# Statistics of x by sums on ScalarE, gate and value products in two-part form, v spread a step later

## The chip, the cores and the metric

One NeuronCore of a Trainium2 chip. The metric is the device time of one execution in microseconds. The kernel before was run three times: 274.16, 274.37 and 275.07 us, median 274.37 us.

## What is computed

x is (4, 1024, 256) in fp32. One layer of linear attention and one of a gated channel mix, each on a layer norm:

```python
a = layernorm(x)                                  # no gain, no bias
q = a @ Wq + bq;  k = (a @ Wk + bk) @ Wc @ We;  v = (a @ Wv + bv) @ Wc @ We
qf, kf = elu(q) + 1, elu(k) + 1                   # 16 heads of 16, 4 heads for k and v
num = qf . cumsum(kf outer v);  den = qf . cumsum(kf) + 1e-6
y = a + (num / den) @ Wo + bo
x2 = x + layernorm(y) * gamma + beta
z = layernorm(x2);  zp = z one token earlier (0 for the first)
xr = mu_r*z + (1-mu_r)*zp;  xk = mu_k*z + (1-mu_k)*zp
out = x2 + sigmoid(xr @ W_r) * (relu(xk @ W_k)**2 @ W_v)
```

## The kernel before

Tokens go in 8 chunks of 128 tokens; a chunk takes the same 128 positions of all 4 batches, so the tiles have 128 tokens on the partitions and 4 x 256 values (or, transposed, 128 of 256 channels on the partitions and 512 tokens). Each engine has its own list of instructions, written out by hand; semaphores tie them together. After a prologue for weights and chunk 0, `step(c)` runs for c = 0 to 6 and `finale(7)` closes. In one step four chunks are in flight:

- n + 1 = c + 2: `norm_x`, the statistics of x (`bn_stats` and `bn_aggr` on DVE, L1053 and L1059), rstd and bias on POOL (L233 to L237), then `normalise_x` on ACT (L890, `a_tok`);
- n = c + 1: `a_tok` is transposed and copied out (`aT`), keys and values (L418, `kb`, `v_half`), the queries (L431, L434), the feature map exp(min(q,0)) on ACT (`eq`, L844 and L846) and its max on DVE (`qf`, L1089), the sums of keys (`ksum`), the products for the denominators on POOL (`prod`, L284);
- c: scores, mask (`probs`, L1125), outputs and division (`oT`, L1137);
- m = c - 1: output projection (L514), residual and statistics of y (`y_tok`), `centre` (L1158), `second_residual` (L1169, writes `x2_tok`), its statistics, then `normalise_z` on ACT (L904);
- f = c - 2: the channel mix: `shift_z` (`zT`), the difference `dz` on POOL (L292), `xr` and `xk` on DVE (L1184), `mix_r` (L536) with `gate_r` (tanh on ACT), `mix_k` (L529) with `channel_k` (relu, square, `ka_high` on ACT), `mix_v_parts` (L567, L571), the gate on DVE (L1197), `finish` on POOL (L299), and the store.

A product of two fp32 matrices is either one fp32 matmul per tile (two instructions each in the trace), or three fp32r matmuls: an operand is split into a high part (a copy that rounds, on ACT) and a low part (operand minus high part, on DVE or POOL), and high x high, high x low and low x high are summed. Before, the queries of chunks 2 to 7, the value product `mix_v` in the steps and for the last chunk, and `mix_r` of the last chunk are done in parts; `mix_r` of the others is fp32.

Steps 0 and 1 are shorter (no channel mix yet). POOL's `add_bo` and `add_beta` (L269, L276) prepare what the residuals add. The middle of a step on ACT, the engine that the change loads, reads

```python
                if n + 1 < NC:
                    normalise_x(n + 1)
                keys(n)
                if f >= 0:
                    gate_r(f, 0, x1)
                ...
                queries(n, 0, x0)
                queries(n, 1, x1)
                values(n)
                state_blocks(n)
```

Here `values(n)` spreads `v_half` over the heads (`v_pad`, four copies), `state_blocks` copies the running state, and `keys_transposed` makes `kfT`, for which the next chunk's first scores wait.

## Time and profile before

| | |
|---|---|
| median of 3 runs | 274.37 us |
| the profiled execution, its own time | 275.64 us |
| its span | 273.9 us |
| granted TensorE clock over the span | 0.994 |
| PE busy | 261.3 us (95%), 3035 matmuls |
| DVE busy | 233.0 us (85%), 561 |
| ACT busy | 164.9 us (60%), 331 |
| POOL busy | 146.4 us (53%), 167 |
| DMA | 10.75 MB, mean 39 GB/s |
| chain that ended last | PE 62%, DVE 20%, ACT 10%, issue 5%, POOL 2% |

Times in the rows are microseconds from the start of the span. "busy" is time in which an engine works on an instruction; the chain that ended last is the row of instructions, each released by the one before it, that leads to the end. PE's matmuls overlap, so starts are read rather than durations. Step 0 lies at about 23 to 43 us, step 1 to 65, step 2 to 98, steps 3 to 6 follow at about 30 us each, and the finale begins at 219 us.

### The profile page before, as it was taken

The page shows a single profiled execution, that of the slowest core. Times are in us where ns is not written, and L with a number is a line of the kernel's source. Part 1 is how long each engine was busy: PE and PEld are TensorE (multiplying, and loading weights), DVE is VectorE, ACT ScalarE, POOL GpSimd, SP SyncE. Part 2 cuts the span into 40 slices and gives each one's busy share as a digit, 9 for nine tenths or more (in the row PEclk, how much of TensorE's full clock was granted, in tenths as well). Part 3 has the DMA queues.
Part 4 walks back from the last instruction along what each step waited for, and adds up shares of the span by engine and source line. Part 5 has one row for each costly group of instructions (what it writes and reads, how often), then busy time and mean ns, then how long its engine had stood idle before and what let it go on. Part 6 is the DMA issues. An engine that isn't in the chain of part 4 may idle for free.

```text
span 273.9 us, 7728 instructions
## 1 busy us (share of the span) xinstructions
PE 261.3 (95%) x3035; PEld 197.0 (72%) x3035; DVE 233.0 (85%) x561; ACT 164.9 (60%) x331; POOL 146.4 (53%) x167
## 2 busy tenths in 40 slices
PE   7999999999898999999999999999999999999894
PEld 7867657868675588758886688658875777685763
DVE  6759578979799989898999989997899877999494
ACT  2448696695746965486747965586438820354670
POOL 3545495579683678335833686355533624070542
PEclk9889999999999999999999999999999999999999
DMA  5910220000020022000400020001100020000213
GB/s 166 274 66 1 79 67 15 4 2 0 4 77 2 2 90 67 2 1 7 151 0 2 2 79 1 0 5 41 41 0 4 2 79 2 0 0 0 78 41 116
DMA packets 12180, 10.75 MB, mean 39 GB/s; under 512 B 2288, under 2 KB 12144, under 8 KB 12144
## 3 DMA queue, kind: packets, MB, share of 16 engines
q1 hardware_dynamic: 11392, 9.97, 11.5%
q8 instruction: 24, 0.39, 0.6%
q10 hardware_dynamic: 752, 0.30, 0.4%
q14 instruction: 12, 0.10, 0.1%
HBM read 6.07 MB, written 4.19 MB: 37 GB/s over the span
## 4 chain that ended last, share of the span: by engine, by line
PE 62%; DVE 20%; ACT 10%; issue 5%; POOL 2%; DVEq 0%; POOLq 0%; ACTq 0%
PE ps_x L514 7%; PE ps_x L529 7%; PE ps_x L536 6%; PE ps_x L418 5%; PE ps_z L485 5%; PE ps_y L501 4%; PE ps_y L506 4%; PE ps_x L567 4%; DVE xk L1184 4%; PE ps_z L589 3%; DVE stats L1053 3%; DVE qf L1089 2%; PE ps_x L522 2%; ACT eq L844 2%; PE ps_x L571 2%
## 5 line engine op out<-in xcount | busy, mean ns | idle before, releaser
L1125 DVE TENSOR_TENSOR probs<-ps_z,causal 128x1024 f32<-128x1024 f32 x32 | 38.7, 1210 | 2.5 <-PE ps_z L485 2.2
L276 POOL TENSOR_TENSOR xb_tok<-x_in,beta_bc 128x1024 f32<-128x1024 f32 x8 | 19.5, 2443 | 20.7 <-DVE x_tok L1169 20.7
L514 PE MATMUL ps_x<-wo_sb,oT 128*128 128x256 f32 x128 | 30.0, 382 | 0.0
L299 POOL TENSOR_TENSOR out_tok<-tanh_r,x_tok 128x512 f32<-128x512 f32 x14 | 18.3, 1315 | 20.1 <-DVE tanh_r L1197 19.8
L284 POOL TENSOR_TENSOR prod<-qf,ksum 128x1024 f32<-128x1024 f32 x7 | 16.5, 2363 | 23.4 <-DVE ksum L1098 23.4
L269 POOL TENSOR_TENSOR abo_tok<-a_tok,bo_bc 128x1024 f32<-128x1024 f32 x8 | 19.1, 2382 | 15.0 <-DVE prod L1118 6.0
L514 PEld LDWEIGHTS ps_x<-wo_sb,oT 128*128 128x128 f32 x128 | 23.4, 190 | 3.6 <-issue 0.5
L485 PE MATMUL ps_z<-qf,kfT 32*128 32x128 f32 x512 | 23.3, 296 | 1.9 <-ACT rden_bc L824 1.1
L229 POOL TENSOR_TENSOR rstd<-rstd,neg_half 128x4 f32<-128x4 f32 x23 | 23.9, 1038 | 1.8
L485 PEld LDWEIGHTS ps_z<-qf,kfT 32*128 32x128 f32 x512 | 17.2, 185 | 7.5 <-issue 3.2
L501 PE MATMUL ps_y<-qf,state 32*32 32x128 f32 x512 | 20.5, 274 | 1.0 <-DVE oT L1137 0.4
L501 PEld LDWEIGHTS ps_y<-qf,state 32*32 32x32 f32 x512 | 11.9, 104 | 12.4 <-issue 9.0
L506 PE MATMUL ps_y<-probs,v_pad 128*32 128x128 f32 x512 | 20.6, 279 | 0.0
L529 PE MATMUL ps_x<-xk,wkT 128*128 128x512 f32 x40 | 18.5, 605 | 1.3 <-DVE qf L1089 1.0
L904 ACT ACTIVATE z_tok<-x_tok,nbias,rstd 128x256 f32<-128x256 f32 x32 | 16.6, 591 | 4.5 <-POOL nbias L237 4.5
L292 POOL TENSOR_TENSOR dz<-zT 128x512 f32<-128x512 f32 x14 | 14.5, 1059 | 7.6 <-ACT zT L824 7.5
L536 PE MATMUL ps_x<-wrT,xr 128*128 128x256 f32 x80 | 18.1, 379 | 0.0
L890 ACT ACTIVATE a_tok<-x_in,nbias,rstd 128x256 f32<-128x256 f32 x24 | 12.5, 590 | 8.7 <-POOL nbias L237 4.4
L418 PE MATMUL ps_x<-wkv_sb,aT 128*128 128x128 f32 x128 | 17.5, 294 | 0.0
L844 ACT ACTIVATE eq<-ps_x,neg_bq 128x512 f32<-128x512 f32 x15 | 10.3, 684 | 11.8 <-PE ps_x L434 11.3
L418 PEld LDWEIGHTS ps_x<-wkv_sb,aT 128*128 128x128 f32 x128 | 16.2, 205 | 0.8
L1089 DVE SCALAR_TENSOR_TENSOR qf<-ps_x,bq,eq 128x512 f32<-128x512 f32 x15 | 11.2, 746 | 6.5 <-ACT eq L846 6.5
(184 smaller groups left out, 668.1 us busy)
## 6 DMA issues: line engine op xcount, KB each, us to landing
x_in<-in_L_attn_x_dram SPq DMA_DIRECT2D x8, 512.0 KB, 4.2
out_dram<-out_tok SPq DMA_DIRECT2D x16, 256.0 KB, 2.1
xr<-in_L_attn_Wq_dram ACTq DMA_DIRECT2D x1, 256.0 KB, 4.2
xk<-in_L_ffn_W_r_dram SPq DMA_DIRECT2D x1, 256.0 KB, 5.1
xk<-in_L_ffn_W_k_dram SPq DMA_DIRECT2D x1, 256.0 KB, 5.3
xr<-in_L_ffn_W_v_dram SPq DMA_DIRECT2D x1, 256.0 KB, 5.6
wo_sb<-in_L_attn_Wo_dram SPq DMA_DIRECT2D x4, 64.0 KB, 4.9
bo_bc<-in_L_attn_bo_dram SPq DMA_DIRECT2D x1, 128.0 KB, 5.3
```

What stands on the lines that cost most here:

```text
L229: PL.tensor_tensor(dst[:], dst[:], neg_half[:], ALU.pow).then_inc(done, 1)
L269: PL.tensor_tensor(abo_tok[n % 2][:], a_tok[n % 2][:], bo_bc[:].unsqueeze(1).to_broadcast([P, NB, D]), ALU.add).then_inc(s_ab, 1)
L276: PL.tensor_tensor(xb_tok[n % 2][:], x_in[n % XBUF][:], beta_bc[:].unsqueeze(1).to_broadcast([P, NB, D]), ALU.add).then_inc(s_xb, 1)
L299: PL.tensor_tensor(out_tok[:, 2 * i:2 * i + 2, :], tanh_r[:, i].rearrange("p (b d) -> p b d", b=2), x2_tok[m % 3][:, 2 * i:2 * i + 2, :], ...
L418: last = mm(x0[:, b * P:(b + 1) * P], aT[:, k, b * P:(b + 1) * P], wkv_sb[:, k, :], start=(k == 0), stop=(k == KD - 1))
L485: last = mm(ps_z[:, g, u * P:(u + 1) * P], kfT[c % 2][rows, 2 * b + u, :, :], qf[c % 2][rows, :, t0:t0 + HALF], start=True, stop=True, ski ...
L501: mm(ps_y[rows, off + u * P:off + (u + 1) * P], state[rows, slot, b, :, :], qf[c % 2][rows, :, t0:t0 + HALF], start=(u == 0), stop=False, ...
L506: last = mm(ps_y[32 * g:32 * g + 32, off + u * P:off + (u + 1) * P], v_pad[c % 2][:, b, u, g, :, :], probs[b % 2][:, g, u * P:(u + 1) * P] ...
L514: last = mm(bk_[:, (b % 2) * D:(b % 2 + 1) * D], oT[m % 2][:, a, b, :], wo_sb[:, a, :], start=(a == 0), stop=(a == 1))
L529: last = mm(bk_[:, :], wkT[:, k, n * P:(n + 1) * P], xk[:, k, :, :], start=(k == 0), stop=(k == KD - 1))
L536: last = mm(bk_[:, (b % 2) * D:(b % 2 + 1) * D], xr[:, k, b, :], wrT[:, k, :], start=(k == 0), stop=(k == KD - 1))
L1125: V.tensor_tensor(probs[b % 2][:].rearrange("p g (r s) -> p g r s", s=HALF), ps_z[:, :, 0:2 * P].rearrange("p g (r s) -> p g r s", s=HALF) ...
```

## The change

- **x's statistics.** In steps 2 to 5 (chunks 4 to 7) DVE's `norm_x` goes. ACT makes them: `sums_x`, four copies of x into `a_tok` with an accumulated sum; POOL's `mean_x`; `squares_x`, four `Square` activations with the mean as bias and an accumulated sum, in two pairs; POOL's `scale_x`; then `normalise_x`, now behind the queries. `values` of chunks 3 to 6 moves to the next step, ahead of `sums_x`; step 6 does chunk 7's as before.
- **Two-part products.** `mix_r` of chunks 0 to 4 (now `mix_r_parts`, with `high_xr` on ACT and `low_xr` on DVE, in buffers of their own), `mix_v` of chunk 6, and the queries of chunk 1. `wq_high` and `wq_low` are made in the prologue.
- **Key features.** exp(min(k,0)) is now two activations, relu and exp; DVE's min goes.
- **Denominators.** The addition of 1e-6 moves from DVE to ACT from step 2 on. `prod` is made in two halves and shares `eq`'s buffer.
- **Prologue.** `a_tok` of chunk 1 is scaled on ACT (two rows before, two after `keys(0)`) and no more on DVE; the transposes of chunk 0 stand together.
- **Order.** In step 0 ACT does the keys before `normalise_x` and `kfT` before the state; in steps 2 to 6 DVE does the second query half before the second `xk`; in step 2 the reciprocals are spread before the second half of the projection.
- **Output.** The sum is written into `x2_tok`, `out_tok` goes; SP waits for the store before.
- **Finale.** Chunk 7's `second_residual`, statistics and scale are done in two halves, its transposes stand before `mix_v` of chunk 6, and its `dz` and `xk` alternate.

The diff, its core (indentation cut by 12):

```diff
@@ -90,7 +93,7 @@
-prod = sb("prod", 2, T)
+prod = eq
@@ -104,7 +107,8 @@
-xr_p, wr_split, s_xrh, s_xrl = aT_p, sem("wr_split"), sem("xr_high"), sem("xr_low")
+xr_p = [ctx.enter_context(nc.sbuf_tensor(f"xr_{part}", [P, KD, T], F32R)) for part in ("high", "low")]
+wr_split, s_xrh, s_xrl = sem("wr_split"), sem("xr_high"), sem("xr_low")
@@ -188,8 +193,10 @@
+        if m >= 1:
+            sp.wait_ge(out_stored[i], 16 * m)
 ...
-                     out_tok[:, 2 * i:2 * i + 2, :]).then_inc(out_stored[i], 16)
+                     x2_tok[m % 3][:, 2 * i:2 * i + 2, :]).then_inc(out_stored[i], 16)
@@ -241,6 +248,21 @@
+def mean_x(n):
+    pool.wait_ge(s_a, 4 * n)
+    pool.wait_ge(s_xs, 4 * (n - 3))
+    PL.tensor_tensor(neg_mean0[:], sum0[:], neg_share[:], ALU.mult)
+    PL.tensor_tensor(mean16[:], sum0[:], neg_share16[:], ALU.mult).then_inc(s_nb0, 1)
+
+def scale_x(n):
+    pool.wait_ge(s_xq, 4 * (n - 3))
+    PL.tensor_tensor(rstd0[:], sq0[:], ln_eps[:], ALU.add).then_inc(s_rs0, 1)
+    pool.wait_ge(s_rs0, 2 * n + 1)
+    PL.tensor_tensor(rstd0[:], rstd0[:], neg_half[:], ALU.pow).then_inc(s_rs0, 1)
+    pool.wait_ge(s_rs0, 2 * n + 2)
+    pool.wait_ge(s_nb0, 2 * n + 1)
+    PL.tensor_tensor(nbias0[:], neg_mean0[:], rstd0[:], ALU.mult).then_inc(s_nb0, 1)
+
@@ -281,8 +303,8 @@
-    PL.tensor_tensor(prod[:], qf[n % 2][:], flat(ksum[n % 2]).unsqueeze(1).to_broadcast([P, 2, T]),
-                     ALU.mult).then_inc(s_prod, 1)
+    for a in range(2):
+        PL.tensor_tensor(prod[:, a, :], qf[n % 2][:, a, :], flat(ksum[n % 2]), ALU.mult).then_inc(s_prod, 1)
@@ -294,23 +316,23 @@
         pool.wait_ge(s_gt, 2 * m + i + 1)
-        if m >= 1:
-            pool.wait_ge(out_stored[i], 16 * m)
-        PL.tensor_tensor(out_tok[:, 2 * i:2 * i + 2, :], tanh_r[:, i].rearrange("p (b d) -> p b d", b=2),
+        PL.tensor_tensor(x2_tok[m % 3][:, 2 * i:2 * i + 2, :], tanh_r[:, i].rearrange("p (b d) -> p b d", b=2),
                          x2_tok[m % 3][:, 2 * i:2 * i + 2, :], ALU.add).then_inc(s_out, 1)
 ...
         token_difference(f)
-    if n + 1 < NC:
+    if f < 0:
         norm_x(n + 1)
-    if f == 0:
-        add_beta(n - 1)
     if f >= 0:
 ...
         first_norm(m)
+        if n + 1 < NC:
+            mean_x(n + 1)
         add_beta(n)
+        if n + 1 < NC:
+            scale_x(n + 1)
         denominator_terms(n)
@@ -322,14 +344,13 @@
             add_beta(n)
-            pool.wait_ge(wq_split, 1)
-            PL.tensor_tensor(wq_p[1][:], wq_sb[:], wq_p[0][:].bitcast(F32), ALU.subtract).then_inc(wq_split, 1)
             pool.wait_ge(wr_split, 1)
 ...
             add_bo(n)
+            add_beta(n)
         else:
@@ -343,13 +364,23 @@
-    second_norm(c)
+    for h in range(2):
+        rows = slice(2 * h, 2 * h + 2)
+        pool.wait_ge(s_st2, 8 * c + 4 * h + 4)
+        if h == 0:
+            pool.wait_ge(s_z, 4 * c)
+        PL.tensor_tensor(neg_mean2[:, rows], mv2[:, rows, 0], neg_one[:, rows], ALU.mult).then_inc(s_nb2, 1)
+        PL.tensor_tensor(rstd2[:, rows], mv2[:, rows, 1], ln_eps[:, rows], ALU.add).then_inc(s_rs2, 1)
+        pool.wait_ge(s_rs2, 2 * c + 2 * h + 1)
+        PL.tensor_tensor(rstd2[:, rows], rstd2[:, rows], neg_half[:, rows], ALU.pow).then_inc(s_rs2, 1)
+        pool.wait_ge(s_rs2, 2 * c + 2 * h + 2)
+        pool.wait_ge(s_nb2, 2 * c + 2 * h + 1)
+        PL.tensor_tensor(nbias2[:, rows], neg_mean2[:, rows], rstd2[:, rows], ALU.mult).then_inc(s_nb2, 1)
 ...
-        pool.wait_ge(out_stored[i], 16 * c)
-        PL.tensor_tensor(out_tok[:, 2 * i, :], tanh_r[:, i, 0:D], x2_tok[c % 3][:, 2 * i, :],
+        PL.tensor_tensor(x2_tok[c % 3][:, 2 * i, :], tanh_r[:, i, 0:D], x2_tok[c % 3][:, 2 * i, :],
@@ -389,6 +422,8 @@
+pool.wait_ge(wq_split, 1)
+PL.tensor_tensor(wq_p[1][:], wq_sb[:], wq_p[0][:].bitcast(F32), ALU.subtract).then_inc(wq_split, 1)
@@ -637,10 +672,10 @@
+    pe.wait_ge(s_pr, 8 * c + 2)
+    spread_reciprocals(c, (z0, z1, z2, z3))
 ...
-    pe.wait_ge(s_pr, 8 * c + 2)
-    spread_reciprocals(c, (z0, z1, z2, z3))
@@ -648,27 +683,22 @@
         pe.wait_ge(s_y, 2 * m + (1 if f else 2))
-        mix_r(f, 0, x1)
+        pe.wait_ge(wr_split, 2)
+        mix_r_parts(f, 0, x1)
         pe.wait_ge(s_y, 2 * m + 2)
-        mix_r(f, 1, x2)
+        mix_r_parts(f, 1, x2)
     outputs(c, 0)
 ...
     pe.wait_ge(s_kv, 2 * n + 2)
-    if m >= 0:
-        pe.wait_ge(wq_split, 2)
-        query_parts(n, 0, x0)
-    else:
-        queries(n, 0, x0)
+    pe.wait_ge(wq_split, 2)
+    query_parts(n, 0, x0)
     if f >= 0:
 ...
         pe.wait_ge(ffn_w_sb, 1)
-    if m >= 0:
-        query_parts(n, 1, x1)
-    else:
-        queries(n, 1, x1)
+    query_parts(n, 1, x1)
     outputs(c, 1)
@@ -747,20 +777,20 @@
     pe.wait_ge(s_zT, 2 * m + 2)
+    transpose_z(c, x0, x2)
     pe.wait_ge(s_gt, 2 * f + 1)
-    mix_v(m, 0, x1)
-    transpose_z(c, x0, x2)
+    mix_v_parts(m, 0, x1)
     pe.wait_ge(s_gt, 2 * f + 2)
-    mix_v(m, 1, ps_y)
+    mix_v_parts(m, 1, ps_y)
     pe.wait_ge(s_rl, 2 * m + 1)
 ...
     pe.wait_ge(wr_split, 2)
-    mix_r_parts(0, z2)
+    mix_r_parts(c, 0, z2)
     pe.wait_ge(s_th, 2 * m + 2)
-    mix_r_parts(1, z3)
+    mix_r_parts(c, 1, z3)
     pe.wait_ge(s_gt, 2 * m + 1)
@@ -833,7 +863,9 @@
-    AC.activation(ek[:], kb[:], ACT.Exp).then_inc(s_ek, 1)
+    AC.activation(ek[:], kb[:], ACT.Relu, scale=-1.0).then_inc(s_nk, 1)
+    act.wait_ge(s_nk, n + 1)
+    AC.activation(ek[:], ek[:], ACT.Exp, scale=-1.0).then_inc(s_ek, 1)
@@ -859,6 +892,11 @@
+def guarded_denominators(n):
+    act.wait_ge(s_den_ps, n + 1)
+    act.wait_ge(s_rb_ps, n)
+    copy(rden[:], x0[:, 0:P], bias=DEN_EPS).then_inc(s_den, 1)
+
@@ -880,13 +918,27 @@
-def normalise_x(n):
+def sums_x(n):
+    act.wait_ge(x_loaded[n % XBUF], x_value(n))
+    act.wait_ge(s_aT_ps, 2 * n - 2)
+    act.wait_ge(s_ab, n - 1)
+    act.wait_ge(s_nb0, 2 * n)
+    for b in range(NB):
+        copy(a_tok[n % 2][:, b, :], x_in[n % XBUF][:, b, :], accum_out=sum0[:, b:b + 1]).then_inc(s_xs, 1)
+
+def squares_x(n, rows):
+    act.wait_ge(s_nb0, 2 * n + 1)
+    for b in rows:
+        AC.activation(a_tok[n % 2][:, b, :], x_in[n % XBUF][:, b, :], ACT.Square, bias=mean16[:, b:b + 1],
+                      scale=1.0 / 16, accum_out=sq0[:, b:b + 1]).then_inc(s_xq, 1)
+
+def normalise_x(n, rows=range(NB)):
 ...
-    for b in range(NB):
+    for b in rows:
@@ -923,6 +977,13 @@
+
+def high_xr(m):
+    if m >= 1:
+        act.wait_ge(s_r_ps, 2 * m)
+    for k in range(KD):
+        act.wait_ge(s_xr, 2 * m + k + 1)
+        copy(xr_p[0][:, k, :], xr[:, k].rearrange("p b t -> p (b t)")).then_inc(s_xrh, 1)
@@ -944,37 +1005,58 @@
         copy(flat(wrT), x1[:, :]).then_inc(ffn_w_sb, 1)
+    if c in (0, 2):
+        reciprocals(c)
+    if f >= 0:
+        high_xr(f)
+    for k in range(KD):
+        act.wait_ge(s_aT, 2 * n + k + 1)
+        copy(aT_p[0][:, k, :], aT[:, k, :]).then_inc(s_aTh, 1)
+    if c == 1:
+        reciprocals(c)
+    on_act = 2 <= c and n + 1 < NC
+    if c == 0:
+        keys(n)
+    if c >= 3:
+        values(c)
+    if on_act:
+        sums_x(n + 1)
+    elif n + 1 < NC:
+        normalise_x(n + 1)
     if c >= 1:
-        for k in range(KD):
-            act.wait_ge(s_aT, 2 * n + k + 1)
-            copy(aT_p[0][:, k, :], aT[:, k, :]).then_inc(s_aTh, 1)
-    if c <= 2:
-        reciprocals(c)
-    if n + 1 < NC:
-        normalise_x(n + 1)
-    keys(n)
+        keys(n)
     if f >= 0:
         gate_r(f, 0, x1)
+    if on_act:
+        squares_x(n + 1, (0, 1))
     if c == 1:
 ...
     if c == 0:
-        copy(flat(wq_p[0]), flat(wq_sb)).then_inc(wq_split, 1)
         act.wait_ge(ffn_w_sb, 1)
 ...
         gate_r(f, 1, x2)
+    if on_act:
+        squares_x(n + 1, (2, 3))
     queries(n, 0, x0)
     queries(n, 1, x1)
-    values(n)
-    state_blocks(n)
+    if on_act:
+        normalise_x(n + 1)
+    else:
+        values(n)
     if c == 0:
 ...
         copy(flat(wkT), x1[:, :]).then_inc(ffn_w_sb, 1)
+        keys_transposed(n)
+    state_blocks(n)
     if f >= 0:
 ...
         channel_k(f, 1, x0, True)
-    keys_transposed(n)
+    if f >= 0:
+        guarded_denominators(n)
+    if c >= 1:
+        keys_transposed(n)
     if c == 0:
@@ -993,15 +1075,13 @@
-    channel_k(m, 0, z0)
-    channel_k(m, 1, z1)
+    channel_k(m, 0, z0, True)
+    channel_k(m, 1, z1, True)
 ...
-    for k in range(KD):
-        act.wait_ge(s_xr, 2 * c + k + 1)
-        copy(xr_p[0][:, k, :], xr[:, k].rearrange("p b t -> p (b t)")).then_inc(s_xrh, 1)
+    high_xr(c)
@@ -1027,8 +1107,12 @@
+act.wait_ge(wq_ready, 1)
+copy(flat(wq_p[0]), flat(wq_sb)).then_inc(wq_split, 1)
+normalise_x(1, (0, 1))
 ...
+normalise_x(1, (2, 3))
@@ -1105,10 +1189,11 @@
-    dve.wait_ge(s_den_ps, n + 1)
-    if n >= 1:
-        dve.wait_ge(s_rb_ps, n)
-    V.tensor_scalar(rden[:], x0[:, 0:P], DEN_EPS, None, ALU.add).then_inc(s_den, 1)
+    if n < 3:
+        dve.wait_ge(s_den_ps, n + 1)
+        if n >= 1:
+            dve.wait_ge(s_rb_ps, n)
+        V.tensor_scalar(rden[:], x0[:, 0:P], DEN_EPS, None, ALU.add).then_inc(s_den, 1)
@@ -1158,13 +1243,13 @@
-def second_residual(m):
+def second_residual(m, rows=range(NB)):
 ...
-        dve.wait_ge(s_out, 2 * m - 4)
-        dve.wait_ge(s_z, 4 * m - 8)
-    for b in range(NB):
+        dve.wait_ge(out_stored[0], 16 * (m - 2))
+        dve.wait_ge(out_stored[1], 16 * (m - 2))
+    for b in rows:
@@ -1203,19 +1287,18 @@
         reciprocal(0)
-    if n + 1 < NC:
+    if f < 0:
         norm_x(n + 1)
-    if f < 0:
         short_step(c, n, m)
 ...
         add_residual(m, 0, x1)
-        add_residual(m, 1, x1)
     token_shift(f, 0, *for_r)
 ...
         add_residual(m, 0, x1)
-        add_residual(m, 1, x2)
+    low_xr(f)
+    add_residual(m, 1, x2 if f else x1)
     mask(c, 1)
@@ -1226,8 +1309,8 @@
     token_shift(f, 0, *for_k)
+    queries(n, 1, x1)
     token_shift(f, 1, *for_k)
-    queries(n, 1, x1)
     divide(c, 1)
@@ -1243,8 +1326,16 @@
-        dve.wait_ge(s_aTh, 2 * n - 3 + k)
+        dve.wait_ge(s_aTh, 2 * n - 1 + k)
 ...
+
+def low_xr(m):
+    if m >= 1:
+        dve.wait_ge(s_r_ps, 2 * m)
+    for k in range(KD):
+        dve.wait_ge(s_xrh, xr_value(m) - 1 + k)
+        V.tensor_tensor(xr_p[1][:, k, :], xr[:, k].rearrange("p b t -> p (b t)"), xr_p[0][:, k, :].bitcast(F32),
+                        ALU.subtract).then_inc(s_xrl, 1)
@@ -1260,8 +1351,10 @@
     else:
-        keys_values(n)
+        keys_values(n, (0,))
         mask(c, 1)
+        keys_values(n, (1,))
+        low_a(n)
     key_features(n)
@@ -1306,19 +1399,24 @@
-    second_residual(c)
-    second_stats(c)
+    for h in range(2):
+        rows = (2 * h, 2 * h + 1)
+        second_residual(c, rows)
+        if h == 0:
+            dve.wait_ge(s_nb2, 2 * c)
+        dve.wait_ge(s_x2, 4 * c + 2 * h + 2)
+        row_stats(x2_tok[c % 3], stats2, s_st2, 8 * c, rows)
+        row_means(stats2, mv2, s_st2, 8 * c + 4 * h, rows)
+    low_part(m, 0)
+    low_part(m, 1)
 ...
-    token_difference(c)
-    token_shift(c, 0, *for_k)
-    token_shift(c, 1, *for_k)
+    for k in range(KD):
+        token_difference(c, k)
+        token_shift(c, k, *for_k)
 ...
-    for k in range(KD):
-        dve.wait_ge(s_xrh, k + 1)
-        V.tensor_tensor(xr_p[1][:, k, :], xr[:, k].rearrange("p b t -> p (b t)"), xr_p[0][:, k, :].bitcast(F32),
-                        ALU.subtract).then_inc(s_xrl, 1)
+    low_xr(c)
@@ -1369,7 +1466,6 @@
-norm_x_scale(1)
```

How the lists read. ACT in step 4 (chunk 4 in attention, statistics for chunk 6) from the high part of aT to the last eq. Before:

```order
L824 ACTIVATE aT_high<-aT 128x512 x2
L890 ACTIVATE a_tok0<-x_in0,nbias0,rstd0 128x256 x4
L836 ACTIVATE ek<-kb 128x256
L824 ACTIVATE v_half<-v_half 64x4x64
L931 ACTIVATE tanh_r<-ps_x1 128x512
L824 ACTIVATE kf<-kf 128x16x16
L931 ACTIVATE tanh_r<-ps_x2 128x512
```

After, the same stretch:

```order
L854 ACTIVATE aT_high<-aT 128x512 x2
L854 ACTIVATE v_pad0<-v_half 64x4x4x16 x4
L854 ACTIVATE a_tok0,sum0<-x_in0 128x256 x4
L866 ACTIVATE ek<-kb 128x256
L868 ACTIVATE ek<-ek 128x256
L854 ACTIVATE v_half<-v_half 64x4x64
L992 ACTIVATE tanh_r<-ps_x1 128x512
L932 ACTIVATE a_tok0,sq0<-x_in0,mean16 128x256 x2
L854 ACTIVATE kf<-kf 128x16x16
L992 ACTIVATE tanh_r<-ps_x2 128x512
L932 ACTIVATE a_tok0,sq0<-x_in0,mean16 128x256 x2
```

The scaling of x has left, and v_pad, the sums, the squares and a second activation for ek have come in.

ACT in step 4 behind the queries. Before:

```order
L844 ACTIVATE eq<-ps_x1,neg_bq 128x512
L846 ACTIVATE eq<-eq 128x512
L824 ACTIVATE v_pad1<-v_half 64x4x4x16 x4
L824 ACTIVATE state<-tail1,row_mask 128x4x16 x4
L920 ACTIVATE k_act<-ps_x1 128x512
L922 ACTIVATE k_act<-k_act 128x512
```

After:

```order
L877 ACTIVATE eq<-ps_x1,neg_bq 128x512
L879 ACTIVATE eq<-eq 128x512
L942 ACTIVATE a_tok0<-x_in0,nbias0,rstd0 128x256 x4
L854 ACTIVATE state<-tail1,row_mask 128x4x16 x4
L974 ACTIVATE k_act<-ps_x1 128x512
L976 ACTIVATE k_act<-k_act 128x512
```

v_pad's place between the queries and the state is taken by the scaling of x, which needs nbias from POOL.

POOL in step 4, from the token difference to the products for the denominators. Before:

```order
L292 TENSOR_TENSOR dz<-zT 128x512 x2
L233 TENSOR_TENSOR neg_mean0<-mv0,neg_one 128x4
L227 TENSOR_TENSOR rstd0<-mv0,ln_eps 128x4
L229 TENSOR_TENSOR rstd0<-rstd0,neg_half 128x4
L237 TENSOR_TENSOR nbias0<-neg_mean0,rstd0 128x4
L269 TENSOR_TENSOR abo_tok1<-a_tok1,bo_bc 128x1024
L227 TENSOR_TENSOR rstd1<-mv1,ln_eps 128x4
L229 TENSOR_TENSOR rstd1<-rstd1,neg_half 128x4
L276 TENSOR_TENSOR xb_tok1<-x_in2,beta_bc 128x1024
```

After:

```order
L314 TENSOR_TENSOR dz<-zT 128x512 x2
L291 TENSOR_TENSOR abo_tok1<-a_tok1,bo_bc 128x1024
L234 TENSOR_TENSOR rstd1<-mv1,ln_eps 128x4
L236 TENSOR_TENSOR rstd1<-rstd1,neg_half 128x4
L254 TENSOR_TENSOR neg_mean0<-sum0,neg_share 128x4
L255 TENSOR_TENSOR mean16<-sum0,neg_share16 128x4
L298 TENSOR_TENSOR xb_tok1<-x_in2,beta_bc 128x1024
L259 TENSOR_TENSOR rstd0<-sq0,ln_eps 128x4
L261 TENSOR_TENSOR rstd0<-rstd0,neg_half 128x4
L264 TENSOR_TENSOR nbias0<-neg_mean0,rstd0 128x4
```

nbias of x stood ahead of abo_tok; it now stands behind xb_tok.

## Rows read from the trace of the kernel before

**Rows 1.** Stretches: busy time (and count) of PE, PEld, DVE, ACT, POOL; clock, DMA
```profile
68.00:98.70 30.70, 28.20 (x355) 20.39 (x353) 27.65 (x65) 20.94 (x43) 18.51 (x18) 1.00 0.06 19
129.00:159.30 30.30, 30.10 (x371) 22.84 (x370) 28.06 (x69) 20.42 (x41) 17.45 (x18) 1.00 0.11 36
```

**Rows 2.** The chain that ended last, step 4: start, duration, what
```profile
128.35 0.66 PE ps_z L485 x16
...
137.89 3.46 PE ps_x L536 x16
...
153.86 0.44 DVE oT L1137
...
155.55 0.67 PE ps_x L567 x4
...
158.61 0.66 PE ps_z L485 x16
```

**Rows 3.** Timeline of ACT, step 4: start, duration, instructions [idle before]
```profile
138.66 0.42 ACT L836 ACTIVATE ek<-kb 128x256 f32<-128x256 f32 x1 [1.12 <-DVE kb L1075]
...
144.77 0.69 ACT L844 ACTIVATE eq<-ps_x,neg_bq 128x512 f32<-128x512 f32 x1 [2.56 <-PE ps_x L434]
...
147.39 1.72 ACT L824 ACTIVATE v_pad<-v_half 64x256 f32<-64x256 f32 x4
149.45 1.06 ACT L824 ACTIVATE state<-tail,row_mask 128x64 f32<-128x64 f32 x4 [0.35 <-DVE tail L1104]
150.97 0.60 ACT L920 ACTIVATE k_act<-ps_x 128x512 f32<-128x512 f32 x1 [0.45 <-PE ps_x L529]
...
154.07 0.63 ACT L824 ACTIVATE ka_high<-k_act 128x512 fp32r<-128x512 f32 x1
```

**Rows 4.** Timeline of DVE, step 4
```profile
130.34 1.39 DVE L1053 BATCH_NORM_STATS2 stats<-x_in 128x6 f32<-128x256 f32 x4
...
132.07 1.88 DVE L1184 SCALAR_TENSOR_TENSOR xr<-dz,mu_r_col,zT 128x512 f32<-128x512 f32 x2
...
140.45 0.28 DVE L1080 TENSOR_SCALAR ek<-ek 128x256 f32<-128x256 f32 x1
...
141.19 1.29 DVE L1247 TENSOR_TENSOR aT_low<-aT,aT_high 128x512 fp32r<-128x512 f32 x2
142.40 1.67 DVE L1169 SCALAR_TENSOR_TENSOR x_tok<-y_tok,rstd,xb_tok 128x256 f32<-128x256 f32 x4
...
146.16 0.75 DVE L1089 SCALAR_TENSOR_TENSOR qf<-ps_x,bq,eq 128x512 f32<-128x512 f32 x1 [0.63 <-ACT eq L846]
```

**Rows 5.** Timeline of POOL, step 4
```profile
130.69 2.04 POOL L292 TENSOR_TENSOR dz<-zT 128x512 f32<-128x512 f32 x2 [0.17 <-ACT zT L824]
132.69 0.65 POOL L233 TENSOR_TENSOR neg_mean<-mv,neg_one 128x4 f32<-128x4 f32 x1
...
144.14 2.39 POOL L276 TENSOR_TENSOR xb_tok<-x_in,beta_bc 128x1024 f32<-128x1024 f32 x1 [4.40 <-DVE x_tok L1169]
...
153.47 0.20 POOL L227 TENSOR_TENSOR rstd<-mv,ln_eps 128x4 f32<-128x4 f32 x1
153.76 1.02 POOL L229 TENSOR_TENSOR rstd<-rstd,neg_half 128x4 f32<-128x4 f32 x1
```

**Rows 6.** Timeline of ACT, prologue and step 1
```profile
17.94 0.69 ACT L844 ACTIVATE eq<-ps_x,neg_bq 128x512 f32<-128x512 f32 x1 [0.40 <-PE ps_x L424]
...
53.87 2.07 ACT L896 ACTIVATE y_tok<-y_tok,nbias,rstd 128x256 f32<-128x256 f32 x4
```

**Rows 7.** Timeline of PE, steps 0 and 2
```profile
41.72 0.73 PE L485 MATMUL ps_z<-qf,kfT 32*128 32x128 f32 x16 [0.43 <-ACT kfT L824]
...
88.43 3.70 PE L529 MATMUL ps_x<-xk,wkT 128*128 128x512 f32 x8 [1.00 <-DVE qf L1089]
```

**Rows 8.** Timeline of PE and of DVE, finale
```profile
260.04 3.67 PE L529 MATMUL ps_z<-xk,wkT 128*128 128x512 f32 x8 [0.99 <-DVE xk L1184]
...
257.94 1.29 DVE L1190 TENSOR_TENSOR dz<-zT 128x512 f32<-128x512 f32 x2 [3.91 <-ACT zT L824]
```

69 lines of the change are left out of this document (38 added, 31 removed).

## The prediction

> **What bounds the kernel now.** I read the stretches first, to see which engine has room. In steady step 4 PE is busy for 30.1 of 30.3 us, DVE for 28.1, ACT for 20.4 and POOL for 17.5; in step 2 PE is busy for 28.2 of 30.7 [rows 1]. So two engines are nearly full, and ACT has some 10 us of room. The chain of waits then says what a step's length is made of: from one `scores(n,0)` at 128.35 to the next at 158.61 it is 30.26 us, almost all PE, with a detour over ACT and DVE in the middle and one over the division `oT` at 153.86 ahead of the last outputs [rows 2]. PE is the bound, but DVE has one idle gap of 0.63 us in the first 17 us of the step, before `qf` [rows 4]. A gain on PE beyond about that is worth what DVE, ACT and POOL let through. The timelines of ACT, DVE and POOL in step 4 are read for that: what is free, what waits for whom [rows 3 to 5]. The prologue, step 2 and the finale bind elsewhere: ACT's `eq` releases `qf` after the prologue's queries, in step 2 PE stands 1.00 us for DVE's `qf`, in the finale 0.99 us for `xk` [rows 6 to 8].
>
> I forecast the difference by positions in the profiled execution (275.64 us; span 273.9) and apply it to the median, 274.37, which lies 1.27 below.
>
> **Steady steps 3, 4, 5, in step 4's times.**
>
> PE: 16 instructions of `mix_r` take 3.46 us in the chain. The value product in parts, same shape, 24 instructions, takes from 155.55 to 158.61, 3.06 [rows 2]. Gain 0.40 a step, if nothing is in the way.
>
> DVE loses x's statistics (1.39 and some 0.35 for the means, [rows 4]) and min (0.28, with a wait 0.4). It gains `low_xr`, priced like `aT_low`, 1.29. But the 1.7 us at the front are not all won: `xr` needs `dz`, whose two halves end at about 131.7 and 132.7 [rows 5]. So the second `xr` ends at 133.5 instead of 133.95 (from 132.07, 1.88, [rows 4]), and 1.3 us of `low_xr` follow. The mask of block 1 and `kb` come 0.9 late, `kf` and `aT_low` 0.5, and `second_residual` ends at 144.5 instead of 144.07. The idle 0.63 before `qf` then swallows the rest: `qf` 0 starts at about 145.95, 0.2 earlier than now. From there to the division that releases the last outputs nothing changes but the order of `qf` and `xk`. DVE alone would thus let a step end 0.0 to 0.3 us earlier, not 0.40.
>
> ACT gains `xr_high` 2 x 0.6, a second activation for `ek` (0.42), the addition for the denominators (about 0.25), and eight passes over x. No row shows an activation with an accumulated sum. The lower bound is a plain one of this size, 2.07 / 4 = 0.52 a piece, less overlap [rows 6]; `v_pad` is 0.43 a piece [rows 3]. An upper bound is one and a half times that, 0.75. I take 0.52, since the arithmetic per element is that of the row. Then ACT runs: aT_high to 135.3, v_pad to 137.0, sums to 139.0, keys (`kb` is there at 139.5) to 140.65, tanh to 141.2, squares, kf, tanh and squares to 144.4, and the first `eq` can start at 144.4, where PE releases it at 144.77 - 0.4 [rows 3]. It just fits. This is 6 us of added work at a cost of nothing, covered by ACT's idle 1.12 before `ek` and 2.56 before `eq` [rows 3] and others; without that cover each 0.1 us lands on `qf` directly.
>
> The Trainium skill (ScalarE: Activation LUTs, Rules for kernel authors) says that relu, max, min and add belong on VectorE, not on ScalarE. By that rule the moved min and addition are a loss; here the row has 0.28 on DVE and 0.42 on ACT, so the rule agrees in size, but in steps 3 to 6 the trace gives ACT room for it.
>
> POOL and ACT behind the queries: this is where I see the loss. `normalise_x` now stands between the queries and the state copies, and waits for nbias. `scale_x` stands behind `xb_tok` on POOL, and `xb_tok` starts when `second_residual` ends: 144.14 now, right after 144.07 [rows 4, 5]. After the change: x_tok ends 144.5, `xb_tok` 144.55 to 147.0. Then an addition (0.20), pow (1.02) and a product (0.20) with gaps, 1.6 us [rows 5], give 148.6. But the small ones are slower when DVE works from SBUF: 0.65 instead of 0.20 beside `xr` [rows 5]. The addition falls beside `xk`, so I take 148.6 to 149.4, middle 149.0. ACT then does four scalings, 2.07 [rows 6], to 151.1, the state (1.06, less overlap 1.0) to 152.1, and the chain from `k_act` to `ka_high`, 150.97 to 154.70 [rows 3], 3.7 us, to 155.7. Before it was done at 154.70. `mix_v_parts` waits for it: 155.7 instead of 155.55, and the second `ka_low` (0.64) comes after it, while PE needs it 0.55 after its start: another 0.1 to 0.2. So a step is 0.1 to 0.7 longer: I take **+0.35 us, three times, +1.05**.
>
> The Trainium skill (SBUF — State Buffer, SBUF: two separate sides) says that VectorE with two SBUF inputs and GpSimd lock each other out for a whole instruction. By it `xk`, wanted at 146.6, would wait for `xb_tok`'s end at 147.0, and POOL's addition for `xk`; nbias would come at 149.3 and the step would be 0.5 longer. The row of 0.65 agrees.
>
> **Step 2.** No statistics of x on DVE, `low_xr` instead, and the second `y_tok` only after it; `centre` no longer beside POOL's two long additions. I place the start of `mix_k`, now 88.43 after 1.00 us of standing [rows 7], 1.5 us earlier. But `xb_tok`, `scale_x`, `normalise_x`, state and `channel_k` follow as above: second residual 83.35, `xb_tok` 85.8, nbias 87.8, `ka_high` 94.6. PE's value product starts at 94.96 in the same timeline before, and at 94.7 to 95.0 after. **-0.1.**
>
> **Step 6** has no statistics of x. PE's 0.40 are the limit, DVE has `low_xr` more and min less: **-0.4.**
>
> **Prologue and steps 0, 1.** ACT does, between `keys(0)` and `queries(0)`, two scalings (1.04) and the relu (0.42). It ended `v_half` at 17.54 and started `eq` at 17.94, released by PE [rows 6]. Now it is free at 16.73 + 0.42 + 0.42 + 0.32 + 1.04 = 18.9, less overlap 18.8: +0.86 on `qf`, and all of it on the chain, as `qf`, `ksum`, `qf` and `prod` follow each other on DVE. In step 0 some comes back: no `wq_high` ahead of `eq`, and `kfT` ahead of the state (1.06), which counts since `kfT` releases `scores(1,0)` at 41.72 [rows 7]. I come to 42.2: **+0.5.** In step 1 relu and exp of the keys stand ahead of the scaling of y at 53.87 on ACT [rows 6], which the chain goes through: **+0.4.**
>
> **Finale.** `mix_k` of the last chunk waited 0.99 us for `xk` to 260.04; `dz` took 257.94 to 259.23, then both `xk` [rows 8]. Now chunk 7's z is scaled in halves, its last transpose is done at about 256.5 instead of 257.3, and the first `xk` needs only the first `dz`. `mix_v` of chunk 6 in parts costs ACT 1.3 and DVE 1.3, both beside other work, and ends at 259.35. So `mix_k` starts at 259.4: **-0.6.** The store is behind the last sum as before; SP's new wait is for a store that is 2 us old by then.
>
> Sum: 0.9 - 0.1 + 1.05 - 0.4 - 0.6 = **+0.85, 275.2 us**. What else moves costs nothing where other work covers it: `prod` in halves (same sum; PE's first denominators start earlier, not the last), the queries of chunk 1 in parts (PE was not last in step 0), the sum in place (the store read the same bytes).
>
> **The rivals.**
>
> *It becomes faster, since ACT and POOL are not last.* If POOL's three small instructions run undisturbed and the plain copies overlap better than I count, nbias comes at 148.4 and `ka_high` at 155.1, and DVE's `oT` sets the step: -0.3 each in steps 3 to 5, -1.0 in step 2. Sum 0.9 - 1.0 - 0.9 - 0.4 - 0.6 = -2.0: **272.4**. It decides the sign as soon as `ka_high` ends before PE's last outputs, some 155.1. For it speaks ACT's 10 us of room [rows 1], against it that the chain over POOL has no slack at all in my count.
>
> *No change.* nbias at 148.6, steps 3 to 5 at 0.0 to +0.15, step 2 at -0.3: **274.2**.
>
> *Accumulated sums cost more.* At 0.75 a piece, sums and squares take 1.8 us more, of which 0.5 hides before `kb`; `eq` comes 0.8 to 1.3 late, and so does everything behind `qf`. Four steps at +0.9 instead of the above: **278**. For it: no row shows the price.
>
> *The stored chunks hold DVE up.* `second_residual` now waits for the store of the chunk three earlier. That store is asked for at the end of step m - 1 and lands some 2 us later, while it is needed 15 us into a later step; I give it 0.02 within the last case.
>
> **Chances.** Forecast case 0.40 (own range 274.7 to 276.5; a quarter of it lies below 275.19), no change 0.22, faster 0.26, costly sums 0.12. A measurement of this kernel can tell about 0.3% from no change, that is 273.55 to 275.19. So slower 0.30 + 0.12 = 0.42, within 0.10 + 0.21 = 0.31, faster 0.26 + 0.01 = 0.27 (0.01 of the no-change case lies below 273.55). Range: from the faster case to most of the costly one, 272.2 to 277.4.
>
> **What would show it.** In the new timeline: ACT's `a_tok` with nbias in step 4 idles for POOL for about 2 us behind the last `eq` (right), or starts at once (the faster rival). `ka_high` ends some 27 us after the step's mask starts at 129.2, now 25.5 after. `eq` of the first query half released by PE (right) or straight behind a square (costly sums; also their mean above 0.6 us). `mix_r` 0.4 shorter. The first `qf` after the prologue at 20.2 instead of 19.32. `mix_k` of the last chunk without its 0.99 of idle. The prediction is wrong if the steps 3 to 5 are shorter than 30.2 us.

## The result and the profile after

| | before | changed |
|---|---|---|
| median of the runs timed together | 274.71 us (274.16 to 275.07) | 278.63 us (278.38 to 278.73) |
| ratio, 95% interval | | 1.0142 (1.0120 to 1.0164) |
| profiled execution, its span | 275.64, 273.9 us | 278.73, 276.3 us |

Slower by 3.9 us, where I had forecast 0.85 slower and a range that ended at 277.4. The starts of `scores(c, 0)` on PE give the time by step:

| | prologue | 0 | 1 | 2 | 3 | 4 | 5 | 6 | finale |
|---|---|---|---|---|---|---|---|---|---|
| before | 22.86 | 18.86 | 21.45 | 34.85 | 30.26 | 30.26 | 30.26 | 30.25 | 54.86 |
| changed | 21.52 | 18.45 | 21.88 | 35.08 | 31.35 | 31.33 | 31.33 | 30.30 | 55.08 |
| difference | -1.34 | -0.41 | +0.43 | +0.23 | +1.09 | +1.07 | +1.07 | +0.05 | +0.22 |

So 3.2 us lie in steps 3, 4 and 5. The busy time of the changed kernel's steps 2 and 4 (us; PE, PEld, DVE, ACT, POOL; clock), beside [rows 1]:

```profile
67.00:97.60 30.60, 28.07 (x362) 20.07 (x359) 26.04 (x58) 23.75 (x58) 19.36 (x19) 1.00 0.06 19
129.00:160.30 31.30, 29.86 (x378) 22.63 (x377) 27.08 (x60) 25.32 (x61) 18.55 (x20) 1.00 0.12 36
```

PE is no longer full: it has 29.9 us of work in 31.3, DVE 27.1, ACT 25.3. The step has become longer than any engine's work, so waits make it. The chain of waits of step 4, where [rows 2] had almost only PE:

```profile
131.84 0.94 DVE xr L1269
...
135.32 1.19 DVE xr_low L1337 x2
136.51 0.61 DVE y_tok L1233
...
137.27 2.39 POOL abo_tok L291
...
140.89 0.45 POOL neg_mean L254
141.33 1.95 POOL mean L255
...
145.19 0.98 ACT a_tok L932 x4
146.17 0.58 ACT eq L877
...
155.41 0.64 PE ps_y L536 x16
```

It runs over DVE, POOL (`mean`), ACT (the squares, then `eq`) and reaches PE only at the end. POOL, step 4 (start, duration, instruction, [idle before]):

```profile
140.89 0.45 POOL L254 TENSOR_TENSOR neg_mean<-sum,neg_share 128x4 f32<-128x4 f32 x1
141.29 1.98 POOL L255 TENSOR_TENSOR mean<-sum,neg_share 128x4 f32<-128x4 f32 x1
144.88 2.37 POOL L298 TENSOR_TENSOR xb_tok<-x_in,beta_bc 128x1024 f32<-128x1024 f32 x1 [1.60 <-DVE x_tok L1254]
...
148.58 0.33 POOL L264 TENSOR_TENSOR nbias<-neg_mean,rstd 128x4 f32<-128x4 f32 x1
```

DVE at the same time, beside [rows 4]:

```profile
131.84 2.09 DVE L1269 SCALAR_TENSOR_TENSOR xr<-dz,mu_r_col,zT 128x512 f32<-128x512 f32 x2 [1.42 <-POOL dz L314]
133.86 0.68 DVE L1233 TENSOR_TENSOR y_tok<-ps_x,abo_tok 128x512 f32<-128x512 f32 x1
...
140.01 1.66 DVE L1243 SCALAR_TENSOR_TENSOR y_tok<-y_tok,mv,gamma_bc 128x256 f32<-128x256 f32 x4
141.59 0.42 DVE L1167 SCALAR_TENSOR_TENSOR kf<-kb,ek 128x256 f32<-128x256 f32 x1
141.93 1.29 DVE L1330 TENSOR_TENSOR aT_low<-aT,aT_high 128x512 fp32r<-128x512 f32 x2
...
147.44 0.75 DVE L1173 SCALAR_TENSOR_TENSOR qf<-ps_x,bq,eq 128x512 f32<-128x512 f32 x1 [1.18 <-ACT eq L879]
```

and ACT, beside [rows 3]:

```profile
137.29 0.42 ACT L854 ACTIVATE a_tok<-x_in 128x256 f32<-128x256 f32 x1
137.61 0.19 ACT L854 ACTIVATION_READ_ACCUMULATOR a_tok<-x_in 128x1 f32 x1
137.70 0.40 ACT L854 ACTIVATE a_tok<-x_in 128x256 f32<-128x256 f32 x1
...
143.31 0.51 ACT L932 ACTIVATE a_tok<-x_in,mean 128x256 f32<-128x256 f32 x1 [1.86 <-POOL mean L255]
...
146.07 0.67 ACT L877 ACTIVATE eq<-ps_x,neg_bq 128x512 f32<-128x512 f32 x1
...
148.99 2.08 ACT L942 ACTIVATE a_tok<-x_in,nbias,rstd 128x256 f32<-128x256 f32 x4 [0.35 <-POOL nbias L264]
...
153.73 0.58 ACT L974 ACTIVATE k_act<-ps_x 128x512 f32<-128x512 f32 x1
```

Three things are to be seen. A POOL instruction on 128x4 elements takes 1.98 us: it begins while DVE goes from `centre` over `kf` to `aT_low` without a gap, and ends at 143.27, about when `aT_low` does. ACT stands 1.86 us for it. And `eq` starts directly behind the last square, not released by PE as at 144.77 before. The price of the sums is not the matter: from one to the next it is 0.40 us, of the squares 0.50, the read of the accumulator (0.19) included.

### The profile page after: what moved, and what is told of

Same layout as the page of the kernel before. It is cut to its first block, busy times and chain, and to the rows that moved or that the text cites. A ratio compares the mean times of both kernels' runs of the same rounds, so it can differ in the third digit from the quotient of the medians.

```text
span 276.3 us, 7926 instructions
## 1 busy us (share of the span) xinstructions
PE 258.0 (93%) x3087; PEld 195.5 (71%) x3087; DVE 228.9 (83%) x523; ACT 191.3 (69%) x426; POOL 153.6 (56%) x184
## 4 chain that ended last, share of the span: by engine, by line
DVE 39%; POOL 18%; PE 17%; ACT 13%; issue 11%; DVEq 0%; POOLq 0%; ACTq 0%
DVE stats L1137 6%; POOL abo_tok L291 4%; DVE ksum L1182 4%; DVE xr L1269 4%; POOL x_tok L319 4%; DVE xk L1269 3%; DVE y_tok L1233 3%; DVE probs L1210 3%; POOL mean L255 3%; PE ps_z L624 3%; ACT a_tok L932 2%; PE ps_x L602 2%; DVE xr_low L1337 2%; POOL dz L314 2%; DVE oT L1222 2%
## 5 line engine op out<-in xcount | busy, mean ns | idle before, releaser
L319 POOL TENSOR_TENSOR x_tok<-tanh_r,x_tok 128x512 f32<-128x512 f32 x14 | 18.3, 1311 | 19.7 <-DVE tanh_r L1281 19.7
L307 POOL TENSOR_TENSOR eq<-qf,ksum 128x512 f32<-128x512 f32 x14 | 17.6, 1278 | 20.1 <-DVE ksum L1182 20.1
L298 POOL TENSOR_TENSOR xb_tok<-x_in,beta_bc 128x1024 f32<-128x1024 f32 x8 | 18.9, 2368 | 10.4 <-DVE x_tok L1254 10.4
L1269 DVE SCALAR_TENSOR_TENSOR xr<-dz,mu_r_col,zT 128x512 f32<-128x512 f32 x16 | 14.7, 960 | 7.3 <-POOL dz L314 7.3
L536 PEld LDWEIGHTS ps_y<-qf,state 32*32 32x32 f32 x512 | 11.9, 104 | 11.2 <-issue 5.5
L236 POOL TENSOR_TENSOR rstd<-rstd,neg_half 128x4 f32<-128x4 f32 x18 | 18.6, 1034 | 1.4
L942 ACT ACTIVATE a_tok<-x_in,nbias,rstd 128x256 f32<-128x256 f32 x28 | 14.6, 589 | 3.4 <-POOL nbias L244 2.1
L854 ACT ACTIVATE zT<-ps_x 128x512 f32<-128x512 f32 x16 | 8.7, 595 | 11.8 <-PE ps_x L557 11.7
L541 PEld LDWEIGHTS ps_y<-probs,v_pad 128*32 128x32 f32 x512 | 12.0, 109 | 6.3 <-issue 6.1
L453 PE MATMUL ps_x<-wkv_sb,aT 128*128 128x128 f32 x128 | 16.4, 281 | 0.0
```

The source lines that it names most:

```text
L236: PL.tensor_tensor(dst[:], dst[:], neg_half[:], ALU.pow).then_inc(done, 1)
L298: PL.tensor_tensor(xb_tok[n % 2][:], x_in[n % XBUF][:], beta_bc[:].unsqueeze(1).to_broadcast([P, NB, D]), ALU.add).then_inc(s_xb, 1)
L319: PL.tensor_tensor(x2_tok[m % 3][:, 2 * i:2 * i + 2, :], tanh_r[:, i].rearrange("p (b d) -> p b d", b=2), x2_tok[m % 3][:, 2 * i:2 * i + 2 ...
L536: mm(ps_y[rows, off + u * P:off + (u + 1) * P], state[rows, slot, b, :, :], qf[c % 2][rows, :, t0:t0 + HALF], start=(u == 0), stop=False, ...
L541: last = mm(ps_y[32 * g:32 * g + 32, off + u * P:off + (u + 1) * P], v_pad[c % 2][:, b, u, g, :, :], probs[b % 2][:, g, u * P:(u + 1) * P] ...
L1269: V.scalar_tensor_tensor(out=dst[:, k], in0=dz[:, k], scalar=mu[:, k:k + 1], in1=zT[:, k, :, 0:P], op0=ALU.mult, op1=ALU.add).then_inc(don ...
```

## The experiments

Position in step 4, in us after its `scores(4, 0)` began, for the kernels the argument rests on (differences of starts read to 0.01 from the timelines; "2nd relu" is the second relu of `k_act`, "step" the length of step 4):

| kernel | kb | mean took | eq | qf | nbias | state | 2nd relu | mix_v | step |
|---|---|---|---|---|---|---|---|---|---|
| before | 9.93 | | 16.49 | 17.88 | 6.90 | 21.17 | 24.51 | 27.20 | 30.26 |
| changed | 11.07 | 1.98 | 17.79 | 19.16 | 20.30 | 22.69 | 25.45 | 28.27 | 31.33 |
| e1, x undone | 11.08 | | 15.90 | 17.90 | 6.90 | 21.43 | 24.21 | 27.24 | 30.30 |
| e2, x alone | 9.93 | 0.64 | 16.50 | 17.89 | 19.60 | 22.10 | 24.87 | 27.22 | 30.28 |
| e8, mix_r undone | 9.93 | 1.98 | 16.65 | 18.02 | 19.20 | 21.56 | 24.38 | 27.14 | 30.21 |
| e3, mean on ACT | 11.07 | ACT | 15.89 | 17.90 | 20.76 | 23.03 | 25.81 | 28.16 | 31.22 |
| e9, beta late | 11.07 | 1.98 | 17.80 | 19.17 | 19.34 | 22.47 | 25.24 | 28.28 | 31.33 |
| e10, both | 11.07 | ACT | 15.90 | 17.89 | 17.74 | 21.19 | 23.97 | 27.01 | 30.08 |
| e11, both on POOL | 11.07 | 0.20 | 15.89 | 17.89 | 17.75 | 21.19 | 23.98 | 27.01 | 30.07 |

### Which part costs

**e1.** All of x put back in steps 2 to 5: `norm_x` on POOL and DVE, `normalise_x` and `values` where they were.

> The changed kernel with all that concerns x in steps 2 to 5 put back: its statistics on DVE and POOL, its scaling and v_pad where they were; everything else of the change stays. If the loss lies in x's statistics on ACT, by whatever mechanism, steps 3 to 5 (start to start of scores(c, 0)) fall from 31.3 us to 30.3 or less, and the time from 278.6 to 275.4 or less: 273.8 if the shorter mix_r (0.4 us a step) then shows, 275.4 if it is hidden. If the loss lies in another part (the order of DVE's pieces, mix_r in parts, prod in eq's buffer), it stays above 277.

274.08 us, 0.9975 (0.9960 to 0.9990) of before; steps 3 to 5 at 30.30 to 30.31. Without x's part there is no loss, and nothing of the shorter `mix_r` shows. DVE's `kb` comes at 11.08 as in the changed kernel: the statistics stood in the wait for `dz`.

```profile
128.29 1.40 DVE L1121 BATCH_NORM_STATS2 stats<-x_in 128x6 f32<-128x256 f32 x4
...
130.02 1.87 DVE L1253 SCALAR_TENSOR_TENSOR xr<-dz,mu_r_col,zT 128x512 f32<-128x512 f32 x2
131.82 0.68 DVE L1217 TENSOR_TENSOR y_tok<-ps_x,abo_tok 128x512 f32<-128x512 f32 x1
```

The first `y_tok` stands 5.59 us into the step with the statistics on DVE and 5.58 without (131.82 - 126.23; 133.86 - 128.28). Taking them away won nothing at this point.

**e2.** The kernel before with x's part alone.

```diff
-                if n + 1 < NC:
+                on_act = 2 <= c and n + 1 < NC
+                if c >= 3:
+                    values(c)
+                if on_act:
+                    sums_x(n + 1)
+                elif n + 1 < NC:
                     normalise_x(n + 1)
 ...
-                values(n)
+                if on_act:
+                    normalise_x(n + 1)
```

> The kernel before with only x's part of the change: sums and squares on ACT in steps 2 to 5, the scaling behind the queries, v_pad in the next step. If x's part alone carries the loss: steps 3 to 5 about 31.3 us instead of 30.3, step 6 as before, 278.0 to 279.0 us in all. If it only hurts together with the rest (high_xr's two passes on ACT as well), steps 3 to 5 stay within 0.4 us of 30.3 and the time below 276.5.

277.34 us, 1.0095 (1.0075 to 1.0115): between my two bounds, and neither case holds: steps 3 to 5 are 30.25 to 30.28, step 6 30.25, but step 2 is 36.40, 1.55 longer. (The profiled execution, 276.54 us, is the fastest of six; the median lies 2.4 us above that of before, and what makes the rest is not shown.) In the steady steps x's part alone costs nothing. In step 2, DVE before:

```profile
73.34 1.38 DVE L1184 SCALAR_TENSOR_TENSOR xr<-dz,mu_r_col,zT 128x512 f32<-128x512 f32 x2
...
76.70 3.81 DVE L1158 SCALAR_TENSOR_TENSOR y_tok<-y_tok,mv,gamma_bc 128x256 f32<-128x256 f32 x4
```

and in e2:

```profile
72.70 4.74 DVE L1234 SCALAR_TENSOR_TENSOR xr<-dz,mu_r_col,zT 128x512 f32<-128x512 f32 x2
...
79.15 1.66 DVE L1208 SCALAR_TENSOR_TENSOR y_tok<-y_tok,mv,gamma_bc 128x256 f32<-128x256 f32 x4
```

POOL in e2 at that time:

```profile
71.78 2.36 POOL L294 TENSOR_TENSOR xb_tok<-x_in,beta_bc 128x1024 f32<-128x1024 f32 x1
74.09 2.79 POOL L287 TENSOR_TENSOR abo_tok<-a_tok,bo_bc 128x1024 f32<-128x1024 f32 x1
```

Without x's four small instructions ahead of them on POOL, its two long additions begin 1.7 us sooner in the step (9.26 us after `scores(2, 0)`, 10.92 before), and lie over `xr` instead of `centre`: `xr` is 3.4 us longer and `centre` 2.1 shorter. So the two engines hold each other up in both directions. How much of the 1.55 us this makes was not tested by a run of its own; `kf`, behind both, comes 0.95 us later in the step.

**e4.** The statistics alone put back; the scaling stays behind the queries, `v_pad` in the next step.

> The changed kernel with only the statistics of x back on DVE and POOL; the scaling stays behind the queries and v_pad stays in the next step. If the statistics are what costs and the two moves are free: the same as with all of x put back, within 0.3 us, and eq of step 4 no later than 144.8 by the clock of the kernel before. If the moves cost by themselves (scaling behind the queries keeps k_act and ka_high back, as the prediction had it): steps 3 to 5 0.3 to 0.6 us longer than with all of x put back.

274.09 us, 0.9972 (0.9959 to 0.9985), like e1, `eq` at 15.89. The two moves are free as long as nbias is early (6.90 here); the statistics on ACT cost.

**e8.** The changed kernel with `mix_r` in one fp32 pass again, without `high_xr` and `low_xr`.

> The changed kernel with mix_r of steps 2 to 6 in one fp32 pass again: no high_xr on ACT (1.2 us a step), no low_xr on DVE (1.3), 0.45 us a step more on PE. x's part alone put into the kernel before left steps 3 to 5 at 30.26. If the loss of 1.05 us a step comes from x's part together with the split of xr (ACT's sums 0.7 us and DVE's centre sooner or later against POOL's mean): steps 3 to 5 about 30.3, step 6 30.3, 275.0 to 276.0 us. If not: 31.3 plus up to 0.45, 278.6 to 280.

273.40 us, 0.9958 (0.9944 to 0.9972), faster than the range I gave; steps 30.21. `mean` takes 1.98 us here too, and ACT waits 1.86 for it as in the changed kernel, but in a step in which `kb` stands at 9.93 instead of 11.07 the squares end at 16.66, where PE released `eq` at 16.49 before. The loss is in the sum of two parts: `low_xr` moves DVE's chain 1.14 us back, and with it the place of POOL's `mean`.

A third part of the change is in it, and I had overlooked it. In e2 `mean` starts at the same place of the step as in e8 (11.87), but takes 0.64 us:

```profile
141.04 0.64 POOL L251 TENSOR_TENSOR mean<-sum,neg_share 128x4 f32<-128x4 f32 x1
```

```profile
139.76 1.66 DVE L1208 SCALAR_TENSOR_TENSOR y_tok<-y_tok,mv,gamma_bc 128x256 f32<-128x256 f32 x4
141.34 0.29 DVE L1130 TENSOR_SCALAR ek<-ek 128x256 f32<-128x256 f32 x1
141.74 0.43 DVE L1133 SCALAR_TENSOR_TENSOR kf<-kb,ek 128x256 f32<-128x256 f32 x1
```

The first row is POOL, the others DVE, all of e2. The min on `ek`, with one input, still stands between `centre` and `kf`, and `mean` ends at 141.68, ahead of `kf`; it takes 0.64 in steps 3 and 5 too. In e8, as in the changed kernel, the min has gone to ACT, and `mean` takes 1.98. That the moved min makes the difference is read from these two traces; no run puts it back alone.

### Which wait

**e3.** The squares' mean made by ACT.

```diff
-                PL.tensor_tensor(neg_mean0[:], sum0[:], neg_share[:], ALU.mult)
-                PL.tensor_tensor(mean16[:], sum0[:], neg_share16[:], ALU.mult).then_inc(s_nb0, 1)
+                PL.tensor_tensor(neg_mean0[:], sum0[:], neg_share[:], ALU.mult).then_inc(s_nb0, 1)
 ...
+                act.wait_ge(s_xs, 4 * (n - 3))
+                copy(mean16[:], sum0[:], scale=-1.0 / (16 * D)).then_inc(s_xm, 1)
```

> The changed kernel, but the mean that the squares need is made by ACT itself, one small activation a step behind the sums; POOL makes only the other, negated mean, which the squares do not wait for. Theory A (POOL's second small operation is held up beside DVE's back-to-back operations, 1.98 us for 128x4, and ACT waits 1.86 us for it): the wait goes, eq comes about 1.2 us sooner, steps 3 to 5 fall by 0.8 to 1.1 us, step 2 likewise, 274.7 to 275.5 us. Theory B (what ACT's eight more passes with their reads of the accumulator take, 6 us a step, is what holds eq up wherever the wait stands): within 0.8 us of 278.6. Theory C (the prediction's: nbias late, scaling late, ka_high late, mix_v late): no more than 0.3 us a step from xb_tok starting earlier, 277.5 to 278.6.

278.09 us, 1.0117 (1.0099 to 1.0136). `eq` came 1.9 us sooner, more than theory A said, and the step only 0.1 shorter: A had the wait right and its worth wrong, B had the time right and its reason wrong (e11 below). C, the prediction's own wait for nbias, had the time too, and its wait is the one that is left. So a second wall stood behind the first:

```profile
149.24 2.08 ACT L943 ACTIVATE a_tok<-x_in,nbias,rstd 128x256 f32<-128x256 f32 x4 [2.44 <-POOL nbias L263]
```

```profile
154.63 0.64 PE L493 MATMUL ps_x<-eq,head_cols 128*32 128x128 f32 x16 [1.35 <-ACT k_act L975]
```

The first row is ACT, the second PE. The scaling waits for nbias, the state copies and relu stand behind it, and PE's denominators, 1.7 us ahead of `mix_v`, wait for the second relu.

**e5, e6, e7.** `scale_x` ahead of `add_beta`: with e3's edit (e5), alone (e6), and with `mean_x` ahead of `first_norm` instead of e3's edit (e7). The edit of e6:

```diff
                     if n + 1 < NC:
                         mean_x(n + 1)
+                        scale_x(n + 1)
                     add_beta(n)
-                    if n + 1 < NC:
-                        scale_x(n + 1)
```

> The changed kernel with two edits: the squares' mean made on ACT (as in the run before, where the wait for it went and a wait of 2.44 us for nbias came in its place, the second relu of k_act ended at 154.58 and PE's denominators stood 1.35 us for it), and scale_x ahead of add_beta on POOL. Theory C2 (two walls one behind the other, the mean and then nbias behind xb_tok; either alone hides the other): nbias at about 146.3, the scaling directly behind the last eq at 146.8, state at 149.5, relu released by PE; steps 3 to 5 fall from 31.3 to 30.3 or, since DVE has 2.3 us less to do, to 29.9; 273.0 to 275.0 us. Theory B (the sheer length of ACT's work): no more than 0.3 us a step, 277.0 or more.

> The changed kernel with the second edit alone: scale_x ahead of add_beta on POOL, the means stay on POOL beside DVE. Theory C2: the squares still end at 146.1 and the last eq at 148.6 in step 4, so the scaling can start only 0.35 us sooner than at 148.99: steps 0.2 to 0.4 shorter, 277.0 to 278.2 us. The prediction's theory (nbias behind xb_tok is the whole loss): steps back to 30.3, 274.5 to 275.5.

> Both waits taken away without new work on ACT: on POOL mean_x stands ahead of first_norm, where the sums are ready (139.0) and DVE works from PSUM, and scale_x stands ahead of add_beta. If it is the place of POOL's small operations beside DVE's that makes them long, mean takes 0.2 to 0.65 us instead of 1.98 and the time is within 0.3 us of that of the version with the mean on ACT (273.0 to 275.0). If the small operation is slow wherever it stands, 277 or more.

280.67, 290.77 and 280.81 us (1.0217, 1.0600 and 1.0239): all three expectations failed. nbias came about when I had said (17.75 us into the step in e5 and e7, 19.34 in e6), but `xb_tok`'s long addition now lay over DVE's first `xk`. e6, POOL and then DVE:

```profile
154.58 2.36 POOL L298 TENSOR_TENSOR xb_tok<-x_in,beta_bc 128x1024 f32<-128x1024 f32 x1
```

```profile
154.92 2.56 DVE L1268 SCALAR_TENSOR_TENSOR xk<-dz,mu_k_col,zT 128x512 f32<-128x512 f32 x1
```

0.74 in the changed kernel, 2.56 here: it ends 0.55 us after POOL's (157.49, 156.94), and so it does in e5 and e7, where it takes 2.25. In e6 PE stood 1.11 us, as in the changed kernel, and then 1.94 us more ahead of `mix_k`, and TensorE's granted clock fell from 1.00 to 0.50, the lower of its two levels (1.2 of 2.4 GHz; the stretches of e6, PE's busy time first, the clock third from the end):

```profile
156.00:158.00 2.00, 0.27 (x12) 0.07 (x4) 2.00 (x2) 1.43 (x3) 0.94 (x1) 0.99 0.00 0
158.00:160.00 2.00, 1.80 (x2) 0.84 (x3) 2.00 (x6) 0.63 (x3) 0.00 (x0) 0.50 0.00 0
160.00:162.00 2.00, 2.00 (x4) 0.86 (x3) 2.00 (x7) 0.67 (x3) 1.08 (x1) 0.66 0.00 0
```

so that `mix_k` took 5.25 us instead of 3.70. So 1.8 us more on DVE made 2.9 us a step. In the profiled executions of e5 and e7, where PE stood once, for 1.54 us, `mix_k` took 3.70 and the steps 31.6.

**e9, e10, e11.** nbias early without that collision: `add_beta` to the end of the step, behind `second_norm`. Its result is wanted two steps later.

```diff
                     if n + 1 < NC:
                         mean_x(n + 1)
-                    add_beta(n)
-                    if n + 1 < NC:
                         scale_x(n + 1)
                     denominator_terms(n)
                     second_norm(m)
+                    add_beta(n)
```

> scale_x ahead of add_beta made it 12 us worse, because xb_tok's long addition then lay over DVE's first xk (2.56 us instead of 0.7 to 1.0). Here scale_x stands directly behind mean_x, and add_beta goes to the end of the step, behind second_norm, where DVE reads from PSUM and POOL is free; its result is wanted only in the step after the next. The wait for the mean (1.86 us, POOL's second small operation beside DVE) stays. If the collision was the whole of the 12 us and nbias behind xb_tok is only the second wall: xk back under 1.0 us, the last eq still ends at 148.6 of step 4's times, scaling directly behind it, steps 0.3 shorter than in the changed kernel, 31.0 us; 276.5 to 278.0 us in all.

> The same and the squares' mean on ACT: both walls gone and no long POOL operation over DVE's. Theory C2 (two walls, mean and nbias): scaling directly behind the last eq, at about 146.8; relu released by PE; steps 3 to 5 at 29.8 to 30.2 us (PE has 0.45 less to do than in the kernel before, DVE has room), 272.0 to 273.5 us. Theory B (the length of ACT's work): steps stay at 31 or more, 277 or more.

> Both walls gone with the means left on POOL: mean_x ahead of first_norm, scale_x behind it, add_beta at the end of the step. Within 0.4 us of the version with the mean on ACT if POOL's small operations are short where DVE works from PSUM; the means 0.2 to 0.65 us each.

Medians, with the step's length and the ratio to before:

| | mean beside DVE's chain | mean out of the way |
|---|---|---|
| nbias behind `xb_tok` | 278.63 (changed), 31.33 | 278.09 (e3), 31.22, 1.0117 |
| nbias early | 278.63 (e9), 31.33, 1.0150 (1.0127 to 1.0173) | 273.37 (e10), 30.08, 0.9952 (0.9935 to 0.9969) |

e11, with both means on POOL but ahead of `first_norm`, is 273.55 (0.9961, 0.9945 to 0.9978). Each wall alone costs about as much as both. e9 lies above its range, since with `qf` at 19.17 DVE is late for everything behind it whatever nbias does: its chain of waits runs over `mean`, the squares and `eq`, and from `qf` on over DVE. In e11 the same two instructions, at a time when DVE reads from PSUM:

```profile
136.92 0.20 POOL L254 TENSOR_TENSOR neg_mean<-sum,neg_share 128x4 f32<-128x4 f32 x1
137.07 0.20 POOL L255 TENSOR_TENSOR mean<-sum,neg_share 128x4 f32<-128x4 f32 x1
```

0.20 instead of 0.45 and 1.98. And ACT does all its added work in e11 (25.45 us busy in step 4, 20.42 before), with steps of 30.07: theory B, the length of ACT's work, falls.

### The finale

**e12.** e10 with the last chunk's z in one piece. **e13.** e10 with the finale of before (the sum stays in `x2_tok`). **e14.** e10 with the last transposes between the halves of chunk 6's value product again.

> The version with add_beta late and the mean on ACT, with the last chunk's second normalisation in one piece again (second_residual, statistics, POOL's four small operations, as in the kernel before); the rest of the finale as changed. The stretch from scores(7, 0) to the end was 54.85 us before and 55.06 in the changed kernel, where I had forecast 0.6 us less. If the halves gain what they were to gain elsewhere but lose it on POOL (1.9 us of small operations twice): 54.9 to 55.2, no difference. If they help: 0.5 us longer without them. If they hurt: 0.3 us shorter.

> The version with add_beta late and the mean on ACT, with the whole finale as in the kernel before: z of the last chunk in one piece, its transposes between the two halves of chunk 6's value product, that product in fp32, dz twice and then xk twice. From scores(7, 0) to the end 54.85 us if the finale is independent of the steps ahead; 273.2 us in all, 0.2 below the same version with the changed finale. If the changed finale is worth its 0.6 us on a good order of steps: 55.6.

> The version with add_beta late and the mean on ACT, with the changed finale but the last transposes between the two halves of chunk 6's value product again. PE stood 1.09 us for the second half of z in front of the transposes, with the value product behind them. If the order costs (the first half of the product would have filled this wait): 0.5 to 1.0 us shorter, 54.1 to 54.6 from scores(7, 0), 272.6 us. If the chain is POOL's small operations, z, zT, dz, xk, which does not go through the product (mix_k stood ready at 257.00, the second xk ended at 258.02): no more than 0.2 us shorter.

From `scores(7, 0)` to the end: e10 55.08, e12 55.98, e13 54.82, e14 55.53. In all 273.37, 274.15, 272.78 and 273.74 us. The halves are worth 0.9 us as long as the rest of the finale is the new one: without them the last z ends 38.53 us after `scores(7, 0)` instead of 37.55. But the old finale as a whole is 0.3 us shorter than the new. For e14 both of my cases miss: it is 0.45 longer than e10. Where the halves' gain goes, on POOL in e14 (second half; in e10 the same to 0.02 us):

```profile
250.19 0.55 POOL L370 TENSOR_TENSOR neg_mean<-mv,neg_one 128x2 f32<-128x2 f32 x1
250.70 0.64 POOL L371 TENSOR_TENSOR rstd<-mv,ln_eps 128x2 f32<-128x2 f32 x1
251.42 0.70 POOL L373 TENSOR_TENSOR rstd<-rstd,neg_half 128x2 f32<-128x2 f32 x1
252.20 0.20 POOL L376 TENSOR_TENSOR nbias<-neg_mean,rstd 128x2 f32<-128x2 f32 x1
```

This is 2.2 us, the first two rows beside `low_part`, which the split of the product put there, against 1.7 for all four rows in one go before. In e12, with the four in one go but `low_part` beside them, nbias is done at 36.41 us, no sooner than the second half's in e10 (36.42); in e13, without `low_part`, at 35.67. The last z is ready 37.55 us after `scores(7, 0)` in e10 and 37.78 in e13, and `mix_k(7)` starts at 40.75 and 40.99, but takes 3.92 instead of 3.67, with the second `xk` done at 41.77 instead of 41.51. Which of the remaining pieces makes the last 0.3 us was not tried, and the medians of e10 and e13 differ by 0.6, of which the two finales account for 0.3; the rest is not explained.

**e13 has the lowest median of all:** 272.78 us, 0.9929 (0.9911 to 0.9947) of the kernel before, 5.9 us below the changed one.

## Why the prediction was wrong

By its own steps:

- **mix_r shorter by 0.40.** On PE it is shorter by 0.51: from its first start to that of the next product 3.04 us against 3.55. In the step it is worth 0.18 at most (e10, 30.08), since DVE is next, over which most of e10's chain runs; in e1 nothing, and e8, without it, has the median of e10 (273.40, 273.37).
- **DVE.** Forecast: `xr` ends 0.45 sooner, `kb` 0.9 late. Measured: `y_tok` at the same place (5.58 against 5.59), `kb` 1.14 late. I had seen that `xr` waits for `dz`, and still let the freed time win 0.45 us. The first `xr` lies beside POOL's second `dz` (3.41 to 4.45 of the step) and ends at 4.99 and 5.00, whether it starts at 3.56 (changed) or 3.79 (before); the second follows it.
- **"It just fits ... 6 us of added work at a cost of nothing."** This is the step that failed. The work did fit (4.9 us more in step 4, free in e10 and e11); the wait inside it did not. I priced the sums and squares (0.52 a piece, measured 0.40 and 0.50) and left out POOL's `mean_x` between them. It stands behind `first_norm`, comes while DVE does three operations in a row that read two inputs from SBUF, and costs ACT 1.86 us. `eq` started at 17.79 of the step instead of the 16.1 forecast, `qf` 1.28 late instead of 0.2 early. I had the row of 0.65 instead of 0.20 [rows 5], and used it for `scale_x` only.
- **nbias at 148.6 to 149.4, ka_high at 155.7, +0.35 a step.** nbias came at 148.91 and `ka_high` ended at 155.64, so these positions were right (my own terms add up to 155.8, not 155.7). Without the first wall (e3) they still stand at 149.15 and 155.9, and the step is 31.22: this wall alone is worth 1.0 us against the kernel before, not 0.35. The term was mis-sized because I took `mix_v` as the first to wait. PE's denominators wait for the second relu, and outputs, 1.15 us, stand between them and `mix_v`.
- **The Trainium skill's rule** (SBUF — State Buffer, SBUF: two separate sides: the two engines lock each other out for a whole instruction when VectorE reads two SBUF inputs) was the best guide I had, and I applied it to one place. The traces agree: 0.20 against 1.98 us for one POOL instruction, 0.74 against 2.56 for one of DVE's. They say one thing more: POOL's instruction outlasted `centre`'s end, `kf` and `aT_low`, so it did not get its turn between them; with the min between `centre` and `kf` (e2) it did, after 0.64 us.
- **The rival of 278** had the number and the place (`eq` straight behind a square, 0.8 to 1.3 late), with another cause: not the sums, which are cheaper than I took them. That its 278 came nearest was luck.
- **The rival of the stores** took nothing: DVE goes into `second_residual` without an idle gap in every step from 2 to 6.
- **Step 2, -0.1; +0.23 measured.** The same two walls: with both gone it is 33.82, 1.26 less.
- **Step 6, -0.4; +0.05 measured,** and 30.08 in e9, where all else is as changed but `xb_tok` no longer begins 2 us ahead of `xk` (`xk` 0.75 us instead of 0.96). DVE and POOL again, not PE's 0.40.
- **Prologue and step 0, +0.5; -1.75 measured, most of it not the change's.** In the profiled execution of before, TensorE's granted clock was 0.53 and 0.61 from 12 to 16 us:

```profile
12.00:14.00 2.00, 2.00 (x11) 2.00 (x12) 1.21 (x4) 0.56 (x3) 1.72 (x6) 0.53 0.73 163
14.00:16.00 2.00, 2.00 (x13) 2.00 (x13) 0.24 (x1) 0.00 (x0) 1.57 (x4) 0.61 0.49 172
```

  In e2, which has the same prologue, it was 1.00, and `keys_values(0)` took 2.05 us instead of 3.16. That is 1.1 us of this execution, and most of the 1.27 by which it lay above its median. Others may have it too: of the 78 executions of the kernel before timed beside the experiments, 15 have a mean granted clock of 0.994 like this one, and all of these take 275.46 to 275.85 us, against medians of 274.6 to 274.9; where in them the clock falls is not shown. Without it the two spans differ by 3.5 us, the medians by 3.9. From the start of `keys_values(0)` to `scores(0, 0)` the changed prologue takes 9.46 us against 8.73 in e2: +0.73, where I had said 0.86. It starts those matmuls sooner (11.9 to 12.7 us in 14 profiles, 13.0 and 13.5 with the old prologue, where transposes and the small products alternate), and I had given that nothing. Step 0 came out 0.41 shorter; this return was in the sum, and too small.
- **Step 1, +0.4; +0.43 measured.** Right.
- **Finale, -0.6; +0.2 measured.** The last transposes were to be done at 37.45 us after `scores(7, 0)`; they were done at 38.05. I gave the halves their gain and not the doubled small operations on POOL beside `low_part`.

## What to carry to other kernels

When work moves to an engine with room, follow every hand-over that it adds, the four-element ones first: here 4.9 us of added work on ACT were free, and a product of 128x4 on POOL between two pieces of it was enough to cost 1 us a step (e9), because DVE was reading two SBUF inputs at that moment. Test suspected waits in pairs as well as one by one; two walls in a row each look worthless alone (-0.5 and 0.0 us) and together gave 5.3. And before counting an engine's freed time as won, look at what it waits for next: statistics that stand in a wait are free. A small operation of DVE that reads one input can be worth keeping, as the min between `centre` and `kf` was, if another engine gets its turn there.

## What the runs showed of the hardware that I had not expected

- A POOL instruction can stay out through several DVE instructions (1.98 us, over the rest of `centre`, `kf` and `aT_low`), and a long one of POOL's holds DVE until its end: `xk` takes 2.25 and 2.56 us and ends 0.55 us after it, a pair of `xr` takes 4.74 us.
- The granted clock fell to 0.50 and 0.66 in e6, where PE had stood for 1.11 and 1.94 us, and stayed at 1.00 in e5's profile after 1.54 us; in e6 `mix_k` took 1.55 us longer for it.
- An activation with an accumulated sum brings an instruction of its own, ACTIVATION_READ_ACCUMULATOR, 0.19 us, which lies beside the next activation: 0.40 us from one sum to the next, 0.50 from square to square.
